# Two penalty passes on ScalarE, 8-bit integers in the dense part, and SyncE's issue of the shift, in a decoder layer on one core

## The chip, the cores and the metric

The kernel runs on one core of one Trainium2 chip. The metric is the device time of one execution in microseconds. Three runs of the kernel before took 790.53 to 792.27 us, median 791.49.

## The reference

Four sequences of 512 rows of 256 values go through a decoder layer with norms behind each part. All arithmetic is in 32-bit floats.

```python
g = sigmoid(x @ Wg + bg)                      # one gate per row
res = (1 - zi) * max(1 - zi - zj, 0) + zi * min(1 - zi + zj, 1)      # zi = g, zj = g of the key
scope = clip((s - 2) ** (1 - g) + 2 - abs(i - j), 1e-32, 1)
log_pen = log(max(res * scope, 1e-32))
x = layernorm(x + softmax(q @ k.T / 4 + log_pen) @ v)                # 16 heads of 16
x = layernorm(x + (softmax(q @ kc.T / 4 + mask) @ vc) @ Wo + bo)     # keys, values of ctx
xq = fake_quant(x)              # round(x / scale) to -128..127, one scale of max|x| for all
h = fake_quant(silu(xq @ wg_q.T) * (xq @ wu_q.T))                    # 704 wide, one scale of max|h|
x = layernorm(x + h @ wd_q.T)
```

The weights of the dense part are rounded to 8-bit integers too, with a scale for each row.

## The kernel before

`make_plan` (L127) writes the order of the attention work out by hand. There are 32 groups, each of four heads of one sequence in self attention (`"s"`) or cross attention (`"c"`). Every group has 16 tiles of 128 x 512 scores twice. Once the queries stand on the partitions, and VectorE takes the maximum of each row (`row_max`, L1003; self attention adds the log penalty `lp` first). Once the keys stand on the partitions, with the negated maxima brought in as twelve more rows of the product, and ScalarE takes the exponential (`exponential`, L890). The product with the values is TensorE's again (`context`, L1552).

A step has 16 slots. In step n the row maxima of group n are taken, slots 0 to 7 hold the second half of group n-2's exponentials and slots 8 to 15 the first half of group n-1's. Other jobs are hung on slots: projections (`q`, `k`, `v`), the gate, the penalties, the two layer norms of a sequence, the preparation of weights. Each engine walks the slots in order and does its part of a job some slots late: ScalarE 0, VectorE 2, GpSimd 1, with exceptions (L47 to L50; a `low` part on GpSimd comes 5 slots late). TensorE is three row-max tiles ahead (three banks of PSUM) and has two banks for exponentials.

The shift: when all maxima of group n are taken, GpSimd splits them in three 16-bit parts (`shift`, L714), TensorE turns them (slot 3), ScalarE copies them to `mT` (L863) and then, at slot 4, issues the DMA that spreads `mT` over the four heads of the query stack `QS` (L868). The exponentials of the group begin at slot 8. SyncE issues everything else: it stores the three parts of a projection to memory (`store_parts`, L521), loads the key and query stacks of the next group from there (L537, L549), and fetches inputs. Its queue in a step is: stacks, fetches, stores of the step's parts (L627 to L644).

Penalties: for each sequence b there are four tiles of 128 x 512. VectorE makes each in seven passes (`penalty`, L1056 to L1083), `PEN_OPS` (L212), one job each. The first two are `pen_a = max(w - z, 0) * w` with w = 1 - zi as a scalar for each partition (L1067, L1069), the next two add `zi * min(z + w, 1)` (L1071, L1073), the last three multiply with the scope and bound it (L1075, L1077, L1079). The tiles of sequence 0 lie in the prologue (`PROLOGUE`, L213), twelve more in the steps. ScalarE takes `Ln` of all four at once (L840). In self attention half of the key tiles add the log by TensorE, and for the other half (`MUL_KT`) GpSimd multiplies the exponentials by the penalty (L711).

The last sequence's output projection is taken apart: `first_half` and `second_half` (L1442, L1449), additions (L1212), statistics, GpSimd's inverse deviation (L687), normalising (L1047), and the maximum of |x| (L1230). `whole_max` (L1258) takes a maximum over partitions through TensorE and makes the scale.

The dense part: `quantise_x` (L1272) rounds x in three passes: multiply and bound below, bound above and add the rounding constant, subtract it (L1053, L1054, L1275). TensorE turns the integers, ScalarE copies them (L922). Gate and up products of 128 x 512 are made for 24 tiles; ScalarE takes silu, VectorE multiplies (L1300) except each third tile, which GpSimd does from ScalarE's copy (`by_pool`, L491; L767), and VectorE takes a maximum of each pair (L1293). The hidden values are rounded in four blocks of 512 rows. Block 0 is VectorE's (`round_h`, L1310, three groups of three passes). Blocks 1 and 2 are ScalarE's in two passes (L961, L954) with a clip by VectorE (`clip_h`, L1319), block 3 is rounded by VectorE (L1348) and finished by ScalarE and a clip. Down products (L1637, L1650), scaling, residual and norm follow for each block.

## Time and profile before

| what | value |
|---|---|
| median of three runs | 791.49 us (790.53 to 792.27) |
| the profiled execution's own time | 788.92 us |
| its span in the profile | 787.1 us |
| TensorE (PE) busy | 659.1 us, 84% |
| VectorE (DVE) busy | 606.4 us, 77% |
| ScalarE (ACT) busy | 492.9 us, 63% |
| GpSimd (POOL) busy | 326.2 us, 41% |
| mean granted TensorE clock | 0.947 |
| chain that ended last | PE 42%, DVE 24%, POOL 14%, ACT 10%, issue 8% |

The span runs from the first to the last instruction; the profiled execution took 1.8 us more than it, and 2.57 us less than the median of the runs. All positions are microseconds from the start of the span. PEld is TensorE's loading of weights, SPq and ACTq are instructions of a queue, such as the issue of a DMA. The granted clock is a share of full speed: 1.0 is 2.4 GHz and 0.5 is 1.2 GHz. The prologue ends near 40 us, the 32 steps near 674 us, and the dense part begins near 710 us.

### The profile page before, as it was taken

How to read it: one execution, taken by the hardware profiler on the slowest of the kernel's cores; microseconds unless marked ns; L12 is line 12 of the kernel's file. 1: busy time of each engine (PE TensorE's matmuls, PEld its weight loads, DVE VectorE, ACT ScalarE, POOL GpSimd, SP SyncE). 2: the span in 40 equal slices, each digit the busy share in tenths (PEclk: the TensorE clock that was granted, in tenths of full speed). 3: DMA queues.
4: the chain of work that ended last, by engine and by line, in shares of the span. 5: the costliest groups of instructions: out<-in, count | busy, mean ns of one | idle time of the engine just before them, and what ended most of it. 6: DMA issues, size and time to landing. Idle time of an engine off the chain costs nothing.

```text
span 787.1 us, 10691 instructions
## 1 busy us (share of the span) xinstructions
PE 659.1 (84%) x3350; PEld 265.6 (34%) x3350; DVE 606.4 (77%) x1574; ACT 492.9 (63%) x807; POOL 326.2 (41%) x414
## 2 busy tenths in 40 slices
PE   7078889999889799998899899999888899956763
PEld 3053223434322243343232443443222243323331
DVE  4888995687899876677998666569985987538997
ACT  4524657556657968654478787455577776944773
POOL 6205866466664414644663144556514001000403
PEclk9688999999999999999999999999999999986975
DMA  2830370220413323321205123322313410000003
GB/s 94 198 110 23 104 175 31 69 65 23 129 41 84 83 70 83 84 70 45 68 23 144 43 60 98 102 58 86 87 40 85 99 43 7 3 1 0 2 0 107
DMA packets 35751, 53.85 MB, mean 68 GB/s; under 512 B 5232, under 2 KB 26736, under 8 KB 35696
## 3 DMA queue, kind: packets, MB, share of 16 engines
q1 hardware_dynamic: 33776, 51.61, 24.7%
q10 hardware_dynamic: 1920, 1.57, 1.3%
q8 instruction: 27, 0.44, 0.2%
q14 instruction: 28, 0.23, 0.1%
HBM read 36.91 MB, written 14.68 MB: 66 GB/s over the span
## 4 chain that ended last, share of the span: by engine, by line
PE 42%; DVE 24%; POOL 14%; ACT 10%; issue 8%; DMA 1%; SPq 0%; POOLq 0%; ACTq 0%; DVEq 0%
POOL probs L711 10%; PE ps L1568 10%; DVE dist L1010 7%; PE ps L1544 7%; PE ps L1521 7%; PE ps L1405 5%; PE ps L1508 5%; ACT probs L900 4%; PE ps L1501 2%; DVE pen_a L1073 1%; PE ps L1548 1%; PE ps L1549 1%; POOL parts L742 1%; DVE h_all L1300 1%; DVE stats L1032 1%
## 5 line engine op out<-in xcount | busy, mean ns | idle before, releaser
L1521 PE MATMUL ps<-KS,QS 96*128 96x512 bf16 x512 | 197.4, 388 | 41.8 <-DVE mx L1010 31.0
L900 ACT ACTIVATE probs<-ps 128x512 f32<-128x512 f32 x256 | 148.9, 597 | 122.6 <-PE ps L1549 91.5
L1010 DVE CUSTOM_DVE_ANT_0 dist<-ps,lp 128x512 bf16<-128x512 f32 x256 | 169.2, 685 | 58.5 <-PE ps L1521 52.8
L711 POOL TENSOR_TENSOR probs<-probs,penT 128x512 f32<-128x512 f32 x128 | 169.7, 1346 | 105.6 <-ACT probs L900 105.6
L1544 PE MATMUL ps<-QS,KS 108*128 108x512 bf16 x512 | 195.3, 384 | 14.6 <-ACT probs L900 11.0
L900 ACT ACTIVATE probs<-ps,mask_col 128x512 f32<-128x512 f32 x256 | 167.0, 690 | 43.8 <-PE ps L1544 40.8
L1010 DVE CUSTOM_DVE_ANT_0 dist<-ps,mask_rest 128x512 bf16<-128x512 f32 x192 | 126.2, 684 | 25.8 <-PE ps L1521 25.6
L1521 PEld LDWEIGHTS ps<-KS,QS 96*128 96x128 bf16 x512 | 50.1, 98 | 189.4 <-DVE mx L1010 122.2
L1568 PE MATMUL ps<-probs,v_s 128*32 128x512 f32 x512 | 68.7, 608 | 16.8 <-POOL probs L711 16.8
L1544 PEld LDWEIGHTS ps<-QS,KS 108*128 108x128 bf16 x512 | 49.8, 98 | 91.2 <-ACT probs L900 58.8
L1568 PE MATMUL ps<-probs,v_c 128*32 128x512 f32 x512 | 68.2, 604 | 0.9 <-ACT probs L900 0.9
L737 POOL TENSOR_TENSOR rest<-proj,parts 128x512 f32<-128x512 f32 x32 | 38.2, 1193 | 72.1 <-ACT parts L807 72.1
L721 POOL TENSOR_SCALAR mrest<-mx 128x16 f32<-128x16 f32 x32 | 9.8, 307 | 103.7 <-DVE mx L1010 103.2
L742 POOL TENSOR_TENSOR parts<-rest,parts 128x512 bf16<-128x512 f32 x32 | 37.8, 1182 | 29.0 <-ACT parts L813 29.0
L1548 PE MATMUL ps<-lpT_hi,ident_h 128*128 128x512 f16 x128 | 48.8, 381 | 0.0
L1549 PE MATMUL ps<-lpT_lo,ident_h 128*128 128x512 f16 x128 | 48.5, 379 | 0.0
L1010 DVE CUSTOM_DVE_ANT_0 dist<-ps,mask_row 128x512 bf16<-128x512 f32 x64 | 42.8, 681 | 7.2 <-PE ps L1521 7.1
L693 POOL TENSOR_SCALAR rstd<-mv 128x4 f32<-128x4 f32 x12 | 2.7, 228 | 104.5 <-DVE mv L1038 104.3
L1010 DVE DVE_READ_ACCUMULATOR2_ANT mx<- 128x1 f32 x512 | 41.6, 81 | 0.0
L807 ACT ACTIVATE proj<-ps,bias_qk 128x512 f32<-128x512 f32 x32 | 22.0, 688 | 20.7 <-PE ps L1405 20.0
L813 ACT ACTIVATE parts<-rest 128x512 bf16<-128x512 f32 x32 | 20.1, 629 | 17.1 <-POOL rest L737 17.1
L1568 PEld LDWEIGHTS ps<-probs,v_s 128*32 128x32 f32 x512 | 10.5, 107 | 42.3 <-issue 42.3
(199 smaller groups left out, 957.7 us busy)
## 6 DMA issues: line engine op xcount, KB each, us to landing
parts_qs<-parts SPq DMA_DIRECT2D x8, 384.0 KB, 2.7
parts_ks<-parts SPq DMA_DIRECT2D x8, 384.0 KB, 2.7
KS<-parts_ks SPq DMA_DIRECT2D x16, 192.0 KB, 3.6
QS<-parts_qs SPq DMA_DIRECT2D x16, 192.0 KB, 4.1
parts_kc<-parts SPq DMA_DIRECT2D x8, 384.0 KB, 2.7
KS<-parts_kc SPq DMA_DIRECT2D x16, 192.0 KB, 3.0
parts_qc<-parts SPq DMA_DIRECT2D x8, 384.0 KB, 2.9
QS<-parts_qc SPq DMA_DIRECT2D x16, 192.0 KB, 3.5
```

What stands on the lines that cost most here:

```text
L711: g.tensor_tensor(probs[:, T % NP, :], probs[:, T % NP, :], penT[:, MUL_KT.index(kt), :], ALU.mult)\
L737: g.tensor_tensor(rest[:, :], proj[:, w % 2, :], parts[:, w % 2, place(job[0], 0), :], ALU.subtract)\
L742: g.tensor_tensor(parts[:, w % 2, place(job[1], 2), :], rest[:, :], parts[:, w % 2, place(job[1], 1), :], ALU.subtract)\
L900: s_.activation(probs[:, T % NP, :], ps[:, exp_bank(T), :], ACT.Exp, bias=bias)\
L1010: v.tensor_tensor_reduce(out=unused[:, (TG * n + i) % AHEAD, :], in0=ps[:, MAX_BANKS[(TG * n + i) % AHEAD], :], in1=lp[:, t, :] if kind == ...
L1405: ins = mm(bank(u), W[what + kind][:, k, c * P:(c + 1) * P], src[:, k, :], start=k == 0, stop=k == HC - 1)
L1508: ins = mm(bank(u)[:, tt * H:(tt + 1) * H], src[:, k, (2 * i + tt) * P:(2 * i + tt + 1) * P], w[:, k, :], start=k == 0, stop=k == HC - 1)
L1521: mm(ps[:, MAX_BANKS[(TG * n + i) % AHEAD], :], QS[0:SK, slot, j, t * P:(t + 1) * P], KS[0:SK, slot, j, :], start=True, stop=True).then_in ...
L1544: ins = mm(o, KS[0:SM, slot, j, kt * P:(kt + 1) * P], QS[0:SM, slot, j, :], start=True, stop=not logged)
L1548: mm(o, ident_h[:, :], lpT_hi[:, k, :], start=False, stop=False)
L1549: ins = mm(o, ident_h[:, :], lpT_lo[:, k, :], start=False, stop=True)
L1568: ins = mm(ps[VC * j:VC * (j + 1), PV_BANK, :], V[kind][:, kt, GH * g + j, :], probs[:, (T + j) % NP, :], start=kt == 0, stop=kt == NT - 1)
```

## The change

Penalties: `PEN_OPS` becomes 5. A new job `relu` on ScalarE, one for each tile, makes `pen_r = Relu(w - z)` and then `pen_r * w` in a buffer of its own; VectorE's second pass now adds it, waiting for `relu_made`, and tells `relu_used`. The `relu` job stands in front of its tile's passes, and in the prologue behind the first part of each projection. Shift: the job `load_m` of ScalarE is gone; SyncE issues the DMA between its loads of the stacks and its fetches and stores. Last norm: two of the four first halves of the projection move to slots before the second half; statistics, inverse deviation, normalising and maximum of the last sequence go in two halves. Integers: `x_clip` and `h_clip` are 8-bit tiles; a multiplication writes into them, with rounding and bounds left to the conversion, and a copy makes them bf16, on VectorE for x, block 1 and the first group of block 0, on ScalarE for the rest. The separate clips are gone. Four scalings of `f_scale` become one (`w_scale` is set to 1 at the start). GpSimd takes nine of the 24 gate/up tiles (1, 3, 6, 8, ... 21) instead of eight.

```diff
@@ make_plan, expand
     if what == "pens":
-        return [("pen", rest[0], t, k) for t in rest[1] for k in range(PEN_OPS)]
+        return [job for t in rest[1] for job in
+                [("relu", rest[0], t)] + [("pen", rest[0], t, k) for k in range(PEN_OPS)]]
...
-            at = [(0, ("shift", s.shift)), (3, ("m", s.shift)), (4, ("load_m", s.shift))] + list(at)
+            at = [(0, ("shift", s.shift)), (3, ("m", s.shift))] + list(at)
...
-    add(at=[(2, ("sigmoids",))])
-    add(at=[(0, ("c2T", B - 1, 1)), (1, ("second_half", B - 1))]
-        + [(2, ("last_x1", B - 1, t)) for t in range(NT)] + [(3, ("x2stats", B - 1, t)) for t in range(NT)],
+    add(at=[(2, ("sigmoids",)), (15, ("first_half_of", B - 1, 2))])
+    add(at=[(0, ("c2T", B - 1, 1)), (0, ("first_half_of", B - 1, 3)), (1, ("second_half", B - 1))]
+        + [(2, (what, B - 1, t)) for t in range(NT) for what in ("last_x1", "x2stats")],
         tasks=[(4, 4, ("ln2", B - 1))])
...
-PEN_OPS = 7
+PEN_OPS = 5
...
+       ("gate", 0, 1), ("reach", 0), ("relu", 0, 0),
+       ("k", "s", 0, 0), ("middle", "k", "s", 0, 0), ("low", "k", "s", 0, 0), ("relu", 0, 1),
+       ("q", "s", 0, 1), ("middle", "q", "s", 0, 1), ("low", "q", "s", 0, 1), ("relu", 0, 2),
+       ("k", "s", 0, 1), ("middle", "k", "s", 0, 1), ("low", "k", "s", 0, 1), ("relu", 0, 3)] \
...
         def by_pool(n):
-            return n % 3 == 2
+            return n % 5 in (1, 3) and n < IT * TC - 2
@@ SyncE
+            def load_shift(n):
+                used(sp, unit[("m", n)])
+                sp.dma_start(QS[SK:SM, n % RING, :, :], mT[:, :].unsqueeze(1).broadcast_to((PARTS * GH, GH, S)))\
+                    .then_inc(shift_loaded, 16)
...
                     for n in s.stacks:
                         load_keys(n)
+                    if s.shift is not None:
+                        load_shift(s.shift)
                     store_parts(now)
...
                     for n in s.stacks:
                         load_stack(n)
+                    if s.shift is not None:
+                        load_shift(s.shift)
                 for what, b in s.fetch:
                     fetch(what, b)
                 store_parts([job for job in jobs if job not in now])
@@ ScalarE
+                elif what == "relu":
+                    b, t = job[1:]
+                    k = NT * b + t
+                    wi, r = w_col[:, t:t + 1], pen_r[:, :]
+                    act.wait_ge(gates_made, b + 1)
+                    if t == 0:
+                        used(act, unit[("gate", b, 1)])
+                    if k:
+                        act.wait_ge(relu_used, k)
+                    s_.activation(r, z_row[:, :], ACT.Relu, bias=wi, scale=-1.0).then_inc(relu_step, 1)
+                    act.wait_ge(relu_step, k + 1)
+                    s_.activation(r, r, ACT.Copy, scale=wi).then_inc(relu_made, 1)
...
-                elif what == "load_m":
-                    n = job[1]
-                    used(act, unit[("m", n)])
-                    act.dma_start(QS[SK:SM, n % RING, :, :], mT[:, :].unsqueeze(1).broadcast_to((PARTS * GH, GH, S)))\
-                        .then_inc(shift_loaded, 16)
...
             act.wait_ge(h_scale_made, 1)
-            for tc in range(1, TC - 1):
-                rounded(tc)
-                integers(tc)
-            integers(TC - 1)
+            rounded(0, H_GROUPS[1:])
+            integers(0, H_GROUPS[1:], 0)
+            for tc in range(2, TC):
+                rounded(tc, H_GROUPS)
+                integers(tc, H_GROUPS, 2 + len(H_GROUPS) * (tc - 2))
@@ VectorE
                 if k == 0:
-                    leave(v.tensor_scalar(pen_a[:, :], z_row[:, :], -1.0, wi, ALU.mult, ALU.add))
+                    leave(v.tensor_scalar(pen_b[:, :], z_row[:, :], wi, 1.0, ALU.add, ALU.min))
                 elif k == 1:
-                    leave(v.tensor_scalar(pen_a[:, :], pen_a[:, :], 0.0, wi, ALU.max, ALU.mult))
+                    dve.wait_ge(relu_made, NT * b + t + 1)
+                    v.scalar_tensor_tensor(pen_a[:, :], pen_b[:, :], zi, pen_r[:, :], ALU.mult, ALU.add)\
+                        .then_inc(relu_used, 1)
...
-                link(round_to(x_round[:, rows, :], x2[:, rows, :], scal[:, 6:7]))
-                v.tensor_scalar(xq[:, rows, :], x_round[:, rows, :], -MAGIC, None, ALU.add).then_inc(xq_made, 1)
+                link(v.tensor_scalar(x_clip[:, rows, :], x2[:, rows, :], scal[:, 6:7], None, ALU.mult))
+                v.tensor_copy(xq[:, rows, :], x_clip[:, rows, :]).then_inc(xq_made, 1)
...
+            def integers(tc, which):
+                cols = slice(tc * 512, (tc + 1) * 512)
+                for lo, hi in which:
+                    m = ISZ[lo]
+                    leave(v.tensor_scalar(h_clip[0:m, lo:hi, cols], h_all[0:m, lo:hi, cols], scal[0:m, 8:9], None, ALU.mult))
+                settle()
+                for lo, hi in which:
+                    m = ISZ[lo]
+                    v.tensor_copy(h_int[0:m, lo:hi, cols], h_clip[0:m, lo:hi, cols]).then_inc(h_ints_by_vector, 1)
...
-            round_h()
-            clip_h(1)
-            for lo, hi in H_GROUPS:
-                h = h_all[0:ISZ[lo], lo:hi, (TC - 1) * 512:TC * 512]
-                v.tensor_scalar(h, h, scal[0:ISZ[lo], 8:9], MAGIC, ALU.mult, ALU.add).then_inc(last_h_rounded, 1)
+            integers(0, H_GROUPS[:1])
+            integers(1, H_GROUPS)
...
-                if tc + 2 < TC:
-                    clip_h(tc + 2)
```

## Rows read from the trace of the kernel before

**Rows 1.** Busy time by stretch (one step each): stretch, length, engines, clock, DMA share, GB/s.

```profile
core 0: us, PE busy (x) PEld busy (x) DVE busy (x) ACT busy (x) POOL busy (x), PEclk, DMA share, GB/s
75.00:98.40 23.40, 19.48 (x96) 6.41 (x92) 21.77 (x47) 14.57 (x26) 19.55 (x19) 1.00 0.29 90
...
120.30:140.90 20.60, 19.26 (x91) 8.75 (x92) 12.48 (x35) 13.52 (x23) 14.50 (x17) 1.00 0.07 22
205.50:227.80 22.30, 17.98 (x97) 5.43 (x96) 21.01 (x51) 10.91 (x19) 13.41 (x14) 1.00 0.47 115
227.80:249.10 21.30, 19.47 (x97) 6.43 (x94) 21.27 (x49) 13.79 (x24) 12.18 (x14) 1.00 0.07 22
...
371.50:392.70 21.20, 17.27 (x92) 5.06 (x88) 21.17 (x51) 10.43 (x18) 12.86 (x13) 1.00 0.25 65
392.70:410.60 17.90, 17.10 (x85) 5.97 (x81) 17.03 (x43) 11.91 (x21) 10.11 (x12) 1.00 0.09 26
```

**Rows 2.** Penalty passes: two groups (busy us, mean ns | idle before), one from the timeline.

```profile
L1069 DVE TENSOR_SCALAR pen_a<-pen_a,w_col 128x512 f32<-128x512 f32 x16 | 13.7, 855 | 0.1
...
L1067 DVE TENSOR_SCALAR pen_a<-z_row,w_col 128x512 f32<-128x512 f32 x16 | 10.0, 623 | 0.1
...
30.55 0.48 DVE L1069 TENSOR_SCALAR pen_a<-pen_a,w_col 128x512 f32<-128x512 f32 x1
```

**Rows 3.** Groups of ScalarE: a pass with a scalar per partition, and the table loads.

```profile
L961 ACT ACTIVATE h_all<-h_all,scal 64x512 f32<-64x512 f32 x2 | 1.4, 708 | 0.0
...
L840 ACT ACT_TABLE_LOAD x4 | 5.1, 1283 | 0.1
```

**Rows 4.** Timeline of the prologue's end: start, duration, engine, instruction, idle before it.

```profile
38.16 1.91 ACT L840 ACTIVATE lp<-pen 128x2048 f32<-128x2048 f32 x1 [4.82 <-DVE pen L1079]
```

**Rows 5.** The shift's issue (ns min/median/max), and stack loads and copy in the timeline.

```profile
L868 ACTq DMA_DIRECT2D QS<-mT x32: 789/790/1402, 58.5 to 679.5; - x32
...
558.38 1.35 SPq L555 DMA_DIRECT2D QS<-parts_qc  x3
...
562.11 0.59 ACT L790 ACTIVATE mT<-ps 12x512 bf16<-12x512 bf16 x1 [0.76 <-PE ps L1468]
```

**Rows 6.** Timeline of the last sequence's norm, 703 to 711 us.

```profile
703.91 0.42 DVE L1212 TENSOR_TENSOR x<-ps,x 128x256 f32<-128x256 f32 x1 [0.86 <-PE ps L1459]
704.37 1.41 DVE L1032 BATCH_NORM_STATS2 stats<-x 128x6 f32<-128x256 f32 x4
...
706.59 1.04 POOL L694 TENSOR_TENSOR rstd<-rstd,minus_half 128x4 f32<-128x4 f32 x1
707.66 1.38 DVE L1047 TENSOR_SCALAR x<-x,mv,rstd 128x256 f32<-128x256 f32 x4 [1.47 <-POOL rstd L694]
709.08 1.22 DVE L1230 TENSOR_REDUCE amax<-x 128x1 f32<-128x1024 f32 x1
```

**Rows 7.** Timeline of the x integers: one of three passes, one of four scalings.

```profile
713.20 0.69 DVE L1054 TENSOR_SCALAR x_round<-x_round 128x1024 f32<-128x1024 f32 x1
...
714.80 0.23 DVE L1280 TENSOR_SCALAR f_scale<-w_scale,scal 128x5 f32<-128x5 f32 x1
```

**Rows 8.** Group of VectorE's gate/up tiles of 128 partitions.

```profile
L1300 DVE SCALAR_TENSOR_TENSOR h_all<-ps,f_scale,silu 128x512 f32<-128x512 f32 x14 | 10.2, 744 | 2.2 <-ACT silu L936 2.2
```

**Rows 9.** Timeline of the hidden integers and down products; last, a stretch with its clock.

```profile
750.67 1.28 DVE L1315 TENSOR_SCALAR h_all<-h_all,scal 128x1536 f32<-128x1536 f32 x1
...
756.86 1.21 DVE L1324 TENSOR_SCALAR h_int<-h_int 128x1536 bf16<-128x1536 bf16 x3
757.99 2.33 DVE L1348 TENSOR_SCALAR h_all<-h_all,scal 128x1536 f32<-128x1536 f32 x3
...
759.88 5.78 ACT L954 ACTIVATE h_int<-h_all 128x1536 bf16<-128x1536 f32 x6
760.23 1.21 DVE L1331 TENSOR_TENSOR y<-ps,out_row 128x1024 f32<-128x1024 f32 x1
...
763.19 3.53 PE L1650 MATMUL ps<-downT,h_int 128*128 128x256 bf16 x24 [0.94 <-DVE h_int L1324]
...
768.41 6.09 PE L1650 MATMUL ps<-downT,h_int 128*128 128x256 bf16 x24 [1.70 <-DVE h_int L1324]
...
768.00:772.00 4.00, 3.59 (x15) 1.81 (x16) 3.93 (x12) 2.08 (x4) 0.70 (x3) 0.52 0.18 65
```

More of the change, by code:

```diff
@@ L56 @@
 EPS = 1e-5
+NORMS = 2 * B + 1
 LOW = -3.0e38
@@ L105, in expand @@
             + [("x2stats", *rest, t) for t in range(NT)]
+    if what == "ln2" and rest[0] == B - 1:
+        return [job for half in range(2) for job in
+                [("x2", *rest, t) for t in range(2 * half, 2 * half + 2)] + [("last_x2max", half)]]
     if what == "ln2":
@@ L391, in decoder_layer @@
         pen_made = sem("penalties_made")
+        relu_step = sem("first_terms_half_made")
+        relu_made = sem("first_terms_made")
+        relu_used = sem("first_terms_used")
         lp_made = sem("log_penalties_made")
@@ L685, in _, with inverse_deviation @@
             chain = norms = 0
-            def inverse_deviation():
+            def inverse_deviation(first=0, last=NT - 1):
                 nonlocal norms
@@ L691, in inverse_deviation @@
                 pool.wait_ge(var_made, norms)
[L692 to L694 removed]
+                k, tiles = norms % 2, slice(first, last + 1)
+                link(g.tensor_scalar(rstd[:, k, tiles], mv[:, k, tiles, 1], EPS, None, ALU.add))
+                g.tensor_tensor(rstd[:, k, tiles], rstd[:, k, tiles], minus_half[:, tiles], ALU.pow).then_inc(rstd_made, 1)
             def link(ins):
@@ L744, in do @@
                         .then_inc(parts_made[w % 2], 1)
+                elif job[0] == "x2stats" and job[1] == B - 1:
+                    if job[2] % 2:
+                        inverse_deviation(job[2] - 1, job[2])
                 elif job[0] in ("x1stats", "x2stats") and job[2] == NT - 1:
@@ L1028, in normalise, with statistics @@
                     .then_inc(side_free[u % 2], 1)
-            def statistics(src, t):
+            def statistics(src, t, first=0, last=NT - 1):
                 ins = v.bn_stats(stats[:, t, :], src[:, t, :])
-                if t == NT - 1:
+                if t == last:
                     link(ins)
@@ L1036, in statistics @@
                     norms[0] += 1
-                    for i in range(NT):
+                    for i in range(first, last + 1):
                         ins = v.bn_aggr(mv[:, k, i, :], stats[:, i, :])
@@ L1216, in do @@
                     leave(v.reciprocal(sig[:, :], sig[:, :]))
+                elif what == "x2stats" and job[1] == B - 1:
+                    b, t = job[1:]
+                    settle()
+                    statistics(x1[:, b % 2, :, :], t, t // 2 * 2, t // 2 * 2 + 1)
                 elif what == "x2stats":
                     b, t = job[1:]
-                    if b < B - 1:
-                        used(dve, *[unit[("wo", b, i)] for i in range(NT // 2)])
-                    elif t == 0:
-                        settle()
+                    used(dve, *[unit[("wo", b, i)] for i in range(NT // 2)])
                     statistics(x1[:, b % 2, :, :], t)
+                elif what == "x2" and job[1] == B - 1:
+                    b, t = job[1:]
+                    n = norms[0] - 1 + t // 2
+                    dve.wait_ge(rstd_made, n)
+                    leave(v.tensor_scalar(x2[:, NT * b + t, :], x1[:, b % 2, t, :], mv[:, n % 2, t, 0:1],
+                                          rstd[:, n % 2, t:t + 1], ALU.subtract, ALU.mult))
+                elif what == "last_x2max":
+                    half = job[1]
+                    settle()
+                    tiles = slice(NT * (B - 1) + 2 * half, NT * (B - 1) + 2 * half + 2)
+                    v.tensor_reduce(amax[:, B - 1 + half:B + half], x2[:, tiles, :], AX.XY, ALU.max,
+                                    apply_absolute_value=True).then_inc(x2_max, 1)
                 elif what == "x2":
@@ L1448, in do @@
                         mm(ps[:, WO_BANKS[t], 0:H], c2T[:, 0, t * P:(t + 1) * P], W["o"][:, 0, :], start=True, stop=False)
+                elif what == "first_half_of":
+                    t = job[2]
+                    pe.wait_ge(exp_done, TG * len(groups))
+                    mm(ps[:, WO_BANKS[t], 0:H], c2T[:, 0, t * P:(t + 1) * P], W["o"][:, 0, :], start=True, stop=False)
                 elif what == "second_half":
```

94 lines of the change are left out of this document (36 added, 58 removed), and 3 rows, old and new, of the table PROLOGUE.

## The prediction

> **What bounds the kernel now.** I first cut the attention part into its steps: a new one begins at every sixteenth row maximum of VectorE (L1010), and for each stretch I compare the busy time of the engines with its length [rows 1]. The steps that compute penalties beside the row maxima are VectorE's: 371.5 to 392.7 us is 21.2 us long with VectorE busy 21.17, 205.5 to 227.8 has 21.01 of 22.3, 227.8 to 249.1 has 21.27 of 21.3, while TensorE is busy only 17.3 to 19.5 and ScalarE 10.4 to 13.8. A step without penalties (120.3 to 140.9) turns this round: TensorE 19.26 of 20.6, VectorE 12.48. So VectorE time is worth up to its full length in the eight of 32 steps that hold penalties, and little in a step like the last. Then comes the dense tail from 699 us on (last layer norm, x integers, gate/up loop, hidden integers, last norm), read from the timeline; there a chain of short VectorE passes sets the end, with TensorE, GpSimd and ScalarE fed in between [rows 6 to 9].
>
> **Two penalty passes to ScalarE.** What goes are L1067 and L1069, 16 of each, mean 623 and 855 ns [rows 2]: 1.48 us a tile. One such pass alone takes 0.48 us [rows 2]; the mean is higher, which I put down to GpSimd's work beside it. Added on ScalarE are a Relu and a Copy, each from SBUF with a per-partition scalar. The nearest form in the trace is L961 on 64x512, 708 ns [rows 3]. With the wait between the two I take 1.45 us a tile. Bounds: 1.2 us if each costs no more than the copy of m (0.59 [rows 5]); 1.6 us with a longer wait.
>
> In the prologue (four tiles) ScalarE gets 5.8 us more, minus some 0.7 us of short waits that it fills. Before the Ln it sat idle 4.82 us [rows 4], waiting for the last penalty. That idle time goes, VectorE is done some 5 us earlier, and the Ln starts between 0.5 us earlier and 1 us later: I take 0, and ScalarE replaces VectorE as what is late.
>
> In the loop there are twelve tiles. Two-tile steps lose 2.96 us of VectorE work. Where TensorE had over 3.5 us to spare I count nearly all of it: 2.7 us (205.5), 2.7 (371.5), 2.5 (75.0). The step at 227.8 has TensorE busy 19.47 of 21.3, so 2.0. The step at 392.7, with one tile and TensorE at 17.10 of 17.9, gives 0.9. Three more steps hold one tile each and have VectorE less than full: 0.6 each, under half of 1.48. Sum 12.6. Against it stand twelve pairs of 1.45 us in ScalarE's in-order queue, with exponentials and the q/k copies behind them. TensorE waits for an exponential to give back one of two banks, so a pair can hold it. The cover is that ScalarE is about half idle there [rows 1] and VectorE has three banks of scores in hand; I let 15% through, 2.6 us. Net **10.0 us**. The ends are 17.7 (12 tiles at 1.48, nothing through) and 2 (most of the pair on the path). The new wait of VectorE on `relu_made` stands behind its row maximum; the relu job has its slot one job ahead, plus VectorE's lag of two slots, so it costs nothing unless ScalarE falls four slots behind. ScalarE's own wait on `relu_used` is for a pass that is eight slots old in a two-tile step.
>
> The trace's rows give 0.48 us on VectorE undisturbed against about 0.7 on ScalarE for the same pass. The Trainium skill ("ScalarE: Activation LUTs", rules for kernel authors) says to keep relu and mul on VectorE, which is up to about 3 times faster. By that rule the move is a loss; it is my slower rival below, since the rows say that VectorE is the full engine in these steps.
>
> **SyncE issues the shift.** L868 holds ScalarE's queue 0.79 us, 32 times [rows 5], though most of that lies beside an activation of 0.6 us that is already running. What is left, 0.2 us, makes at most 32 x 0.2 = 6.4 us of ScalarE, on the path only where ScalarE is late: I take **1.0 us**. The same DMA still has to land. In SyncE's queue the wait for the copy of m now stands behind the six stack loads and in front of the fetches and the stores of that step's parts. The loads are long issued by then: in the step at 554.7 the last group of loads starts at 558.38, for 1.35 us, and the copy of m only at 562.11 [rows 5]. Low parts come at slot 5 or later, behind m at slot 3, so stores wait for nothing new; fetches go out up to 8 us later and are used one step or more later. Bounds 0 to 3 us gained; if a shift came late, see the rivals.
>
> **The tail.** (1) Last output projection and norm. Two of the eight halves of the projection run ahead of c2T's second half, and the statistics go in halves. The last addition now ends at 704.33; with less on TensorE in front of it, it is bounded by VectorE's own add plus statistics (0.42 and 0.35, four times), which I put 1.0 us earlier. From there to the end of the maximum at 710.30 stood 1.41 us of statistics, the power on GpSimd (1.04), 1.38 of normalising and 1.22 of maximum [rows 6]. Behind the last addition stays one statistic of four (1.06 less), and half of the normalising and of the maximum (0.69 and 0.61 less): 2.4. Together **3.4 us**.
> (2) x integers: three passes of some 0.7 us become two, and the second chunk releases TensorE, so 2 x 0.69; four f_scale instructions of 0.2 become one, 0.65 [rows 7]. **2.0 us**.
> (3) Gate/up: VectorE makes 15 tiles instead of 16 at 744 ns [rows 8], but the loop's first three slots now give it two tiles instead of three, and it idles there; the rest is 13 tiles and 11 maxima, as before. 0.
> (4) Hidden integers. VectorE had nine passes and the clips and roundings of other rows before the first scaling at 760.23 [rows 9]. Now it has two passes of 1.28 and 1.22 us for one group, then three roundings (2.33 for all) and three copies (about 2.2): 7.1 us from 750.67, so 757.8, and the first down product is there about 758. Gain 2.3. The two clips of 1.21 us between the scalings go too, with 0.3 us that one waits: 2.7. ScalarE makes as many passes as before in an order that ends some 0.7 us later (766.4 for 765.66); from there TensorE needs 6.1 us for the last 24 products [rows 9] at the low clock (0.52 granted in 768 to 772), to 772.5. VectorE wants its second half at 772.8. Just covered. **5.0 us**. The 8-bit passes show nowhere; I take the duration of the float ones. If they ran at the 1.2 us per 1,024 elements of a maximum, the tail would lose 5 us; the other end is no gain over float.
> Tail: 3.4 + 2.0 + 0 + 5.0 = **10.4 us**, between 4 and 12.
>
> **Sum.** 10.0 + 1.0 + 0 + 10.4 = 21.4 us. The profiled execution took 788.92 us (span 787.1 and 1.8 around it), so it would come to 767.5. The median of the runs is 791.49, 2.57 above; from it the same sum gives 770.1.
>
> **Rivals.**
> - *ScalarE takes back much of the relief.* The pair falls between a q/k copy and its middle part, TensorE is held, and the loop gains 3 us instead of 10. For it: ScalarE is the one whose exponentials release TensorE, and in the step at 227.8 it has 13.8 us of work already. Against: half idle elsewhere. 777.1 us.
> - *The relief is worth all of VectorE's time*, 17.7 us, with less disturbance between VectorE and GpSimd besides. For: three steps with VectorE at 94 to 100%. Against: TensorE's 81 to 91% in them. 762.4 us.
> - *Slower: the pair lies wholly on the path.* Place: ScalarE's queue in the penalty steps, exponentials behind the pair, TensorE at its two banks, VectorE's relief eaten by waiting for scores. Price 12 x 1.45 = 17.4 us against 11.4 gained elsewhere: 797.5 us. It decides from 0.95 us of each pair on the path with no relief. Against: TensorE has waited for VectorE, not for ScalarE, in these steps. This is what the rule named above would make of it.
> - *The change does not do what it says*: Relu calls for its own table. A load takes 1,283 ns [rows 3], two a tile make 41 us. Exp, Copy and Identity follow each other in the trace without one, and I hold it for one in a hundred, inside the slower chance. The Trainium skill ("ScalarE: Activation LUTs", table sets) says that relu sits in every set; no row here shows a Relu.
> - *Tail held by TensorE's clock.* Were the low clock to last through the three later down products, each takes 6.1 us instead of 3.5 [rows 9] and point (4) gains nothing: 775.1 us.
>
> **Chances.** Forecast 0.66; ScalarE takes back 0.15; full relief 0.08; clock in the tail 0.06; slower 0.05. A difference under 0.2% (1.6 us) is about what cannot be told from none; almost nothing lies there. Range 760 to 780: from full relief with the tail's upper bound to the first rival with 3 us more lost in the tail. Faster 0.93, same 0.02, slower 0.05.
>
> **What would show it.** In the changed profile: the steps with two tiles near 19 us with VectorE still the fullest engine; Relu and Copy near 0.7 us without a table load; the Ln in the prologue near 38 us with ScalarE busy up to it; TensorE's shift wait not longer; 3.4 us less from the last projection to the maximum of x, 2.0 less to the first gate product, 5.0 less from the scaled `out_row` to the end. Wrong would be: penalty steps as long as before with TensorE waiting for ScalarE, or 8-bit passes over 1 us per 1,024 elements.

## The result, and the profile after

The changed kernel took 782.89 us in the median of four runs (781.85 to 783.49), beside 791.88 for the kernel before: ratio 0.988 (95%: 0.985 to 0.991). Timed again later (change_again below), the ratio was 0.992 (0.990 to 0.995). So it is some 6 to 10 us faster. The forecast was 21.4 us faster, 770.1, with a range of 760 to 780: the result lies above it.

The profiled execution took 781.85 us, with a span of 780.1 (before 787.1). From the start of the last step's row maxima (661.0 before, 663.3 after) to the end it is 9.3 us shorter, for 10.4 forecast. Everything ahead of that point is 2.3 us **longer**, for 11.0 us shorter forecast. The forecast failed in the attention part.

Stretches of the changed kernel, one step each; they answer to [rows 1], in the order 75.0, 120.3, 205.5, 227.8, (the step behind it), 371.5, 392.7:

```profile
core 0: us, PE busy (x) PEld busy (x) DVE busy (x) ACT busy (x) POOL busy (x), PEclk, DMA share, GB/s
76.60:101.10 24.50, 20.11 (x96) 6.57 (x100) 18.85 (x44) 16.68 (x30) 20.21 (x20) 1.00 0.32 99
123.40:144.10 20.70, 19.29 (x91) 8.75 (x92) 12.56 (x37) 13.49 (x23) 14.53 (x17) 1.00 0.22 61
210.10:231.80 21.70, 17.25 (x93) 5.68 (x96) 18.92 (x46) 13.15 (x23) 13.27 (x14) 1.00 0.46 118
231.80:252.10 20.30, 18.58 (x94) 6.12 (x90) 18.10 (x46) 14.78 (x27) 10.81 (x12) 1.00 0.07 22
252.10:269.70 17.60, 16.84 (x88) 5.33 (x88) 14.38 (x42) 15.56 (x27) 7.02 (x10) 1.00 0.44 130
375.50:395.30 19.80, 16.10 (x88) 5.29 (x88) 19.31 (x47) 12.56 (x22) 12.43 (x13) 1.00 0.26 70
395.30:413.90 18.60, 17.80 (x89) 5.96 (x81) 14.81 (x41) 13.10 (x23) 10.08 (x12) 1.00 0.09 26
```

VectorE did get its relief: in the step at 210.1 it is busy 18.92 of 21.7 us, where before it was 21.01 of 22.3. But the step is hardly shorter, and now no engine is full in it. The step at 252.1 holds no penalty and is 1.0 us longer than its counterpart before (16.6 us).

Who waited for whom in two penalty steps, first of the kernel before (205.5 to 249.1), then of the changed one (210.1 to 252.1): total us, times, longest.

```profile
PEld ps L1521 <- DVE mx L1010: 11.6, 15, 1.1
POOL probs L711 <- ACT probs L900: 11.3, 3, 4.1
...
PEld ps L1544 <- ACT probs L900: 2.7, 6, 0.7
```

```profile
POOL probs L732 <- ACT probs L931: 11.5, 4, 3.8
...
PEld ps L1569 <- ACT probs L931: 5.7, 12, 0.9
PE ps L1593 <- POOL probs L732: 3.9, 4, 1.2
...
PEld ps L1546 <- DVE mx L1037: 3.6, 5, 0.8
DVE dist L1037 <- PE ps L1546: 3.5, 7, 0.9
```

TensorE's wait for VectorE's maxima fell from 11.6 to 3.6 us. In its place stand waits for ScalarE's exponentials (up from 2.7 to 5.7) and for GpSimd's multiplies (up from 1.7 to 3.9), and VectorE waits for TensorE (3.5, for 0.9). The new operations, from the page's groups:

```profile
L869 ACT ACTIVATE pen_r<-pen_r,w_col 128x512 f32<-128x512 f32 x16 | 11.6, 722 | 0.5
L867 ACT ACTIVATE pen_r<-z_row,w_col 128x512 f32<-128x512 f32 x16 | 11.5, 716 | 0.0
```

The prologue's end, ScalarE's timeline (answers to [rows 4]):

```profile
30.43 0.71 ACT L867 ACTIVATE pen_r<-z_row,w_col 128x512 f32<-128x512 f32 x1
31.17 0.72 ACT L869 ACTIVATE pen_r<-pen_r,w_col 128x512 f32<-128x512 f32 x1
31.92 5.50 ACT L855 ACTIVATE KS<-own_rows 32x2048 bf16<-32x2048 bf16 x3
37.44 1.28 ACT L877 ACT_TABLE_LOAD   x1
38.74 1.91 ACT L877 ACTIVATE lp<-pen 128x2048 f32<-128x2048 f32 x1
```

ScalarE is busy without a gap up to the Ln; VectorE had made its last penalty at 34.6 us.

The tail, VectorE's and TensorE's timelines (answers to [rows 6, 7, 9]):

```profile
708.21 0.69 DVE L1261 TENSOR_REDUCE amax<-x 128x1 f32<-128x512 f32 x1
...
711.01 0.75 DVE L1314 TENSOR_SCALAR x_clip<-x,scal 128x1024 int8<-128x1024 f32 x1
711.80 0.69 DVE L1315 CAST xq<-x_clip 128x1024 bf16<-128x1024 int8 x1
...
747.65 1.28 DVE L1350 TENSOR_SCALAR h_clip<-h_all,scal 128x1536 int8<-128x1536 f32 x1
748.96 1.23 DVE L1354 CAST h_int<-h_clip 128x1536 bf16<-128x1536 int8 x1
750.11 2.31 DVE L1350 TENSOR_SCALAR h_clip<-h_all,scal 128x1536 int8<-128x1536 f32 x3
752.45 2.15 DVE L1354 CAST h_int<-h_clip 128x1536 bf16<-128x1536 int8 x3
755.76 1.23 DVE L1361 TENSOR_TENSOR y<-ps,out_row 128x1024 f32<-128x1024 f32 x1 [1.17 <-PE ps L1665]
```

```profile
755.59 7.04 PE L1681 MATMUL ps<-downT,h_int 128*128 128x256 bf16 x48
762.96 3.52 PE L1681 MATMUL ps<-downT,h_int 128*128 128x256 bf16 x24 [0.33 <-ACT h_int L988]
```

### The profile page after: what moved, and what is told of

Same layout as the page of the kernel before. It is cut to its first block, busy times and chain, and to the rows that moved or that the text cites. A ratio compares the mean times of both kernels' runs of the same rounds, so it can differ in the third digit from the quotient of the medians.

```text
span 780.1 us, 10707 instructions
## 1 busy us (share of the span) xinstructions
PE 659.0 (84%) x3348; PEld 267.6 (34%) x3350; DVE 574.5 (74%) x1523; ACT 511.0 (66%) x841; POOL 326.4 (42%) x417
## 4 chain that ended last, share of the span: by engine, by line
PE 46%; POOL 16%; DVE 14%; ACT 12%; issue 10%; DMA 2%; SPq 0%; POOLq 0%; DVEq 0%; ACTq 0%
POOL probs L732 12%; PE ps L1593 10%; PE ps L1546 8%; PE ps L1569 8%; PE ps L1533 5%; PE ps L1430 5%; ACT probs L931 5%; DVE dist L1037 4%; PE ps L1526 3%; POOL rest L758 1%; PE ps L1573 1%; PE ps L1574 1%; PE ps L1446 1%; POOL parts L763 1%; DVE x L1214 1%
## 5 line engine op out<-in xcount | busy, mean ns | idle before, releaser
L732 POOL TENSOR_TENSOR probs<-probs,penT 128x512 f32<-128x512 f32 x128 | 167.2, 1325 | 107.9 <-ACT probs L931 107.9
L1037 DVE CUSTOM_DVE_ANT_0 dist<-ps,mask_row 128x512 bf16<-128x512 f32 x64 | 42.9, 683 | 10.4 <-PE ps L1546 10.3
L714 POOL TENSOR_SCALAR rstd<-mv 128x4 f32<-128x4 f32 (+1 forms) x13 | 3.0, 232 | 98.6 <-DVE mv L1065 98.5
L837 ACT ACTIVATE parts<-rest 128x512 bf16<-128x512 f32 x32 | 20.1, 629 | 17.8 <-POOL rest L758 17.8
```

The costliest lines, as they stand in the source:

```text
L732: g.tensor_tensor(probs[:, T % NP, :], probs[:, T % NP, :], penT[:, MUL_KT.index(kt), :], ALU.mult)\
L1037: v.tensor_tensor_reduce(out=unused[:, (TG * n + i) % AHEAD, :], in0=ps[:, MAX_BANKS[(TG * n + i) % AHEAD], :], in1=lp[:, t, :] if kind == ...
```

## The experiments

All were timed in five rounds beside the kernel before; ratios are to it, with 95% intervals. "us" is the median. Where two ratios are compared below, their difference is given in us of the kernel before's 791. Four of the kernels leave work out and so compute something else: relief_alone and loop_relief (a term of the penalty), relief_few_mul and passes7_few_mul (three of four multiplies, the first of them that term too).

| label | us | ratio |
|---|---|---|
| pens_only | 794.75 | 1.0053 (1.0028 to 1.0079) |
| shift_only | 790.01 | 0.9984 (0.9964 to 1.0005) |
| tail_only | 781.82 | 0.9880 (0.9853 to 0.9907) |
| no_pens | 780.74 | 0.9869 (0.9842 to 0.9896) |
| relief_alone | 780.23 | 0.9852 (0.9821 to 0.9884) |
| pair_alone | 783.57 | 0.9910 (0.9878 to 0.9941) |
| passes7_few_mul | 748.80 | 0.9464 (0.9430 to 0.9498) |
| relief_few_mul | 743.18 | 0.9392 (0.9360 to 0.9424) |
| relu_quiet | 785.76 | 0.9932 (0.9905 to 0.9959) |
| half_quiet | 782.53 | 0.9915 (0.9888 to 0.9942) |
| ln_first_quiet | 781.89 | 0.9891 (0.9858 to 0.9924) |
| pens_shift | 793.72 | 1.0035 (1.0019 to 1.0051) |
| ln_first | 783.39 | 0.9898 (0.9880 to 0.9915) |
| seven_ln_first | 779.71 | 0.9871 (0.9848 to 0.9894) |
| prologue_only | 775.44 | 0.9810 (0.9780 to 0.9840) |
| not_batch1 | 780.95 | 0.9861 (0.9839 to 0.9883) |
| loop_relief | 774.18 | 0.9808 (0.9772 to 0.9844) |
| change_again | 785.13 | 0.9924 (0.9900 to 0.9949) |

### The change in its parts

**pens_only**, **shift_only** and **tail_only** add one part to the kernel before; **no_pens** is the changed kernel without the penalty move; **pens_shift** is the kernel before with both attention parts.

```diff
 # no_pens: the first two passes back on VectorE, no relu job
-PEN_OPS = 5
+PEN_OPS = 7
```

> The kernel before with the penalty move alone. Between the two traces the attention part was 2.3 us longer and the tail 9.3 us shorter. Theory 1 (ScalarE's pair lies on the path and takes the relief back, or more): 1 to 4 us slower than before, with PE waiting for probabilities in the penalty steps. Theory 2 (VectorE's relief is worth little, because exponential, GpSimd's multiply and context product set these steps, and the pair costs nothing either): within 1 us of before. The sum on record wanted 10.0 us faster.

> The kernel before with only the issue of the shift's DMA moved to SyncE. Forecast on record: 1.0 us faster (0 to 3). Theory 3 (the shift's move is what costs the attention part its 2.3 us, since it now stands behind loads in SyncE's queue): 2 to 3 us slower. Otherwise within 1 us of before or up to 3 us faster.

> The kernel before with only the dense tail changed (last norm in halves, 8-bit integers, GpSimd's share, one f_scale pass). Sum on record: 10.4 us faster. From the two traces, measured from the start of the last row-maximum step: 9.3 us faster, so about 782.5 us.

> The changed kernel with all seven penalty passes on VectorE again. Theory 1 (pair on the path): 1 to 4 us faster than the changed kernel, 779 to 782 us, better than both. Theory 2 (relief worth nothing, pair free): within 1 us of the changed kernel's 782.9. The sum on record would make it 10 us slower.

> The kernel before with the penalty move and the shift's move, without the tail: the changed kernel's attention part. By itself the penalty move measured 4 us slower and the shift's move 1.3 us faster (790.9 to 790.0 in medians). If they simply add: 793 to 794 us. If the shift's move pays for part of the pair, because its 0.79 us no longer stands in ScalarE's queue near it: 791 to 792.5 us.

The tail is worth 1.2%, 9.5 us: all that the change gains. The shift's move gives 1.3 us, not told from nothing. The penalty move makes the kernel before **slower** by 0.5% (4 us), with the shift's move beside it 0.35%; the changed kernel's two timings (0.9879, 0.9924) lie above no_pens (0.9869), the second clear of its interval, the first not. So the part from which 10 us were expected costs 1 to 4.

### Relief and price apart

```diff
 # relief_alone: no pair on ScalarE, the add reads another buffer
-                [("relu", rest[0], t)] + [("pen", ...
+                [("none", rest[0], t)] + [("pen", ...   # keeps the passes' slots
...
-                    dve.wait_ge(relu_made, NT * b + t + 1)
-                    v.scalar_tensor_tensor(pen_a[:, :], pen_b[:, :], zi, pen_r[:, :], ...)
+                    v.scalar_tensor_tensor(pen_a[:, :], pen_b[:, :], zi, z_row[:, :], ...)
 # pair_alone: the pair stays, VectorE makes seven passes
-PEN_OPS = 5
+PEN_OPS = 7
```

> The changed kernel without the Relu and Copy on ScalarE: VectorE keeps its five passes and adds z_row where the first terms stood, so the penalties leave out the term w_i*max(w_i - z_j, 0). It has VectorE's relief and pays nothing on ScalarE. Measured: 780.74 us with seven passes on VectorE, 782.9 with the change. Theory 1 (ScalarE's pair takes back a relief that is there, as the 12.6 us of the record): 768 to 772 us. Theory 2 (the relief is worth little, since exponential, GpSimd's multiply and context product set these steps): 777 to 781 us, within 3 us of the version with seven passes.

> The changed kernel with the pair on ScalarE kept and VectorE making all seven passes as before, so the pair's result is not used: the price of the pair alone, against 780.74 us without it. Theory 1 (a large relief taken back): 788 to 792 us. Theory 2 (small relief, small price): 781 to 784 us.

Against no_pens the relief alone gives 1.3 us (ratios 0.9869 and 0.9852), the pair alone costs 3.2 us; each lies within the intervals. Both hold the prologue's four tiles too: the first row maximum comes at 36.0 us in relief_alone, at 40.0 in no_pens and at 42.2 in pair_alone. The times are as Theory 2 said of the relief, but they don't even show those 4.0 us of lead; the mean granted clock of relief_alone's runs is 0.945 to 0.951, that of no_pens' 0.949 to 0.953. The traces say more, since a step whose granted clock is 1.00 mostly repeats to 0.1 us: change_again's trace has eight of the changed kernel's nine lengths below again, and 25.7 us for the step at 76.6, where its clock was 0.93. The table has nine steps that hold penalties or stand behind one that does, all at 1.00, lengths in us (by the change's positions; the step at 55.0 is left out, since its clock differs, and those at 123.4 and 413.9, which kept their 20.7 and 18.2 us):

| kernel | 76.6 | 101.1 | 210.1 | 231.8 | 252.1 | 326.2 | 352.4 | 375.5 | 395.3 | sum |
|---|---|---|---|---|---|---|---|---|---|---|
| before | 23.4 | 21.8 | 22.3 | 21.3 | 16.6 | 26.5 | 23.0 | 21.2 | 18.0 | 194.1 |
| relief_alone | 23.2 | 22.3 | 21.4 | 19.9 | 17.6 | 26.1 | 23.0 | 19.7 | 18.5 | 191.7 |
| changed | 24.5 | 22.3 | 21.7 | 20.2 | 17.6 | 26.2 | 23.0 | 19.8 | 18.7 | 194.0 |

The relief is 2.4 us (12.0 forecast in these steps), the pair takes back 2.3 (2.6 forecast), 1.3 of it in the one step at 76.6. Relieved steps do get shorter (231.8: 1.4 us, 375.5: 1.5), but the step behind each gets longer (1.0 and 0.5): the row maxima ran ahead, and then stand and wait. In pair_alone, where VectorE makes all seven passes, the eight steps from 101.1 on sum to 170.6 us, and so they do in no_pens: there the pair costs nothing in the loop at full clock, and 2.2 of its 3.2 us are the prologue's.

So the 2.3 us by which everything ahead of the tail got longer are not in these nine steps (194.1 and 194.0). The first row maximum comes 0.6 us later, the two steps behind it take 1.0 us more at a granted clock of 0.74 for 0.84, and the step at 165.1, without penalties, takes 21.6 us at 0.92 for 20.1 at 1.00; 0.8 us come back at 536.4 and 555.1.

### Is GpSimd's multiply the cap?

```diff
-                if e and groups[e[0]][0] == "s" and e[1] // GH in MUL_KT:
+                if e and groups[e[0]][0] == "s" and e[1] // GH in MUL_KT and e[1] % GH == GH - 1:
```

> relief_alone with three of four multiplies of GpSimd left out (the last of each four is made; the other probabilities go without their penalty). To be held against passes7_few_mul. Theory 2 (GpSimd's multiply stands between the exponential and the context product and caps the penalty steps): with that cap gone VectorE's relief shows, this kernel is 6 us or more faster than passes7_few_mul, and penalty steps get down to 17 to 19 us. Rival (TensorE or ScalarE caps them): under 3 us between the two.

> Seven penalty passes on VectorE, no pair on ScalarE, three of four multiplies of GpSimd left out. Against 780.74 us with all multiplies. Theory 2: VectorE is the only bound left in the penalty steps and they stay near 21 us or shrink only as its passes get shorter without GpSimd beside them; relief_few_mul is 6 us or more below. Rival: both kernels within 3 us of each other.

The two differ by 5.6 us, but the first row maximum alone is 4.4 us earlier in relief_few_mul (35.5 for 39.9). That much is the prologue. The nine steps sum to 175.9 us with seven passes and 173.1 with five: 2.8 us, hardly more than with all multiplies. So the multiplies make these steps 18 us longer, but they are not what makes the relief worthless. Two steps of each, seven passes first:

```profile
196.30:214.80 18.50, 17.03 (x96) 5.21 (x92) 18.07 (x50) 10.69 (x19) 4.54 (x8) 1.00 0.39 95
353.00:371.90 18.90, 17.22 (x96) 5.17 (x88) 18.86 (x51) 10.40 (x19) 4.46 (x8) 1.00 0.27 73
```

```profile
189.60:206.50 16.90, 16.83 (x96) 5.55 (x90) 16.48 (x46) 10.75 (x19) 4.03 (x8) 1.00 0.42 103
344.10:361.50 17.40, 16.71 (x96) 5.34 (x88) 17.37 (x46) 10.45 (x19) 4.07 (x8) 1.00 0.30 79
```

In the step at 189.6 TensorE is busy 16.83 of 16.9 us: where GpSimd is out of the way, TensorE takes over within 1.6 us of the 18.5 with seven passes. In the step at 344.1 VectorE stays the full engine, and there its relief shows whole: 1.5 us less for 1.49 us less of work. My Theory 2 was half right: in most steps there is a next engine close behind, not GpSimd alone.

### Where the pair stands

```diff
 # relu_quiet
-                [("relu", rest[0], t)] + [("pen", rest[0], t, k) for k in range(PEN_OPS)]]
+        return [("pen", rest[0], t, k) for t in rest[1] for k in range(PEN_OPS)]
...
+    for b in range(1, B):
+        for t in range(NT):
+            ... steps[k].items[6].append(("relu", b, t)), or slot 14 or 15 of the step before
```

> The changed kernel with the pair's slots in the loop moved: from slots 0, 7 and 8 (where the exponentials begin that GpSimd multiplies) to slots 6, 14 and 15. Prologue as in the changed kernel. If the pair's price (3 us measured by itself) comes from standing ahead of these exponentials: 1.5 to 3 us faster than the changed kernel's 782.9, and the first two exponentials of the third penalty step stand 0.6 us apart again instead of 1.9. Rival (the price is ScalarE's time itself, wherever it stands, or the prologue's): within 1 us of 782.9.

In the changed kernel the second pair of the step at 76.6 stands behind the first exponentials of a group, where GpSimd waits to multiply:

```profile
94.49 0.74 ACT L867 ACTIVATE pen_r<-z_row,w_col 128x512 f32<-128x512 f32 x1
95.27 0.72 ACT L869 ACTIVATE pen_r<-pen_r,w_col 128x512 f32<-128x512 f32 x1
95.89 0.58 ACT L931 ACTIVATE probs<-ps 128x512 f32<-128x512 f32 x1
```

Moving it did as was asked of these two exponentials (0.6 us apart again) and the kernel got slower, if anything: 785.76 us. The pair now stood ahead of another exponential. The edit did one thing more, which I had overlooked: with the relu jobs gone from the list, the penalty passes were dealt over the slots anew (those of a first tile stand at 0, 1, 3, 4, 6 for 1, 2, 4, 5, 6). The step at 101.1 is 23.5 us for 22.3, but loop_relief below, with the same slots and no pair in the loop at all, has 23.2 there: most of that is the passes' own place. Held against loop_relief, the pair costs 1.5 us in the six steps that are at full clock in both; in its old place it cost 0.9 in the same six (changed kernel against relief_alone). So that the price comes from a bad slot is not borne out; that it is ScalarE's time ahead of exponentials, wherever it stands, is what is left, and not shown by itself.

### The prologue

```diff
 # ln_first (on the change), ln_first_quiet (on relu_quiet), seven_ln_first (on no_pens)
-    + [("own_rows", r) for r in range(1, RING)] \
     + [job for job in expand(("pens", 0, range(NT))) if job[0] == "pen"] + [("ln", 0)] \
+    + [("own_rows", r) for r in range(1, RING)]
 # half_quiet: tiles 0 and 1 of the prologue with seven passes on VectorE
```

> relu_quiet with two tiles of the prologue back on VectorE (seven passes) and two on ScalarE. In the prologue ScalarE then loses 2.9 us ahead of the Ln and VectorE gains some 3; relief_alone had the first row maximum 4.0 us earlier, the change 0.7 us later than seven passes. If ScalarE's queue alone holds the Ln: the Ln comes 2 us or more earlier and the whole is 1.5 to 2.5 us faster than relu_quiet. If not: within 1 us of relu_quiet.

> relu_quiet with the Ln of the prologue ahead of ScalarE's three copies of constant rows (5.50 us together) instead of behind them. In the changed kernel VectorE made its last penalty at 34.6 us and the Ln began at 38.74, straight behind these copies. If that is what turns the prologue's relief into nothing: the Ln begins near 34.7, the first row maximum near 36.7, and the whole is 3 to 4.5 us faster than relu_quiet. Rival (what follows needs the rows, or the exponentials behind the copies start later by as much): within 1 us of relu_quiet.

> The changed kernel with only the prologue's Ln put ahead of the three 1.8 us copies of constant rows. In the quiet-slot version this gave 3.2 us. If the copies held the Ln in the changed kernel: the Ln begins near 34.7 us for 38.74, the whole is 3 to 4.5 us below 782.9, 778.5 to 780. If not: 782 to 784.

> Seven passes on VectorE everywhere, no pair, and the Ln ahead of the constant rows: the control. With seven passes VectorE's last penalty ends near 38.0 us and is what the Ln waits for, so the order on ScalarE should give nothing: 780 to 781.5 us, as the version with seven passes. If the copies by themselves delay something else, 777 to 779.

With the Ln first, the changed kernel's ScalarE and VectorE meet there:

```profile
31.52 1.28 ACT L877 ACT_TABLE_LOAD   x1
34.30 1.91 ACT L877 ACTIVATE lp<-pen 128x2048 f32<-128x2048 f32 x1 [1.51 <-DVE pen L1105]
36.24 5.50 ACT L855 ACTIVATE KS<-own_rows 32x2048 bf16<-32x2048 bf16 x3
```

The Ln begins 4.4 us earlier. That the copies held the Ln is settled by these rows; ln_first_quiet gained 3.2 us on relu_quiet, with intervals that overlap, and the control with seven passes stayed with no_pens (0.9871 and 0.9869), so that there VectorE's last penalty is what is late. half_quiet failed as a test: its second pair stood 3.54 us waiting until VectorE had read the one buffer, so the Ln came at 39.17 us, no earlier; its 1.3 us less than relu_quiet lie within the intervals. But **ln_first** itself gained nothing that can be told from the change (0.9898 beside 0.9879 and 0.9924). In its profile the 5.3 us of lead at the second step are still 5.0 us at the fourth and 6.5 at 263.2, and gone by the last step (0.9 us). Most of it, 4.6 us, goes in two steps that hold no penalty at all, first of the change and then of ln_first:

```profile
536.40:555.10 18.70, 17.36 (x86) 6.28 (x83) 17.76 (x53) 11.19 (x21) 12.09 (x15) 1.00 0.28 90
```

```profile
531.00:554.70 23.70, 20.13 (x90) 7.41 (x87) 23.36 (x51) 13.01 (x23) 15.78 (x17) 0.93 0.23 76
...
554.80:573.70 18.90, 17.24 (x90) 5.53 (x88) 15.29 (x44) 10.03 (x18) 6.15 (x9) 0.91 0.41 100
```

The granted clock fell to half in part of each of ln_first's two. Ahead of the second fall TensorE had stood for 3.00 us behind a row maximum:

```profile
554.28 0.39 PE L1546 MATMUL ps<-KS,QS 96*128 96x512 bf16 x1 [3.00 <-DVE mx L1037]
```

```profile
554.80:558.80 4.00, 4.00 (x16) 0.93 (x15) 1.95 (x8) 0.60 (x1) 0.00 (x0) 0.57 1.03 248
```

From 8 us behind the first row maximum to the last step the traces have three to seven such falls, near 275 us in each kernel with all multiplies, the others not always in the same steps. The scatter of the runs goes with the mean clock: of the eight runs of change_again the fastest is 781.77 us at 0.951 and the slowest 787.67 at 0.943.

### The loop by itself, with the better prologue

All three have ln_first's prologue. **prologue_only** makes seven passes in the loop, **loop_relief** five without a pair, **ln_first** five with the pair; **not_batch1** takes only batch 1's four tiles back.

```diff
+def moved(b, t):
+    return b == 0          # prologue_only;  b != 1 in not_batch1
 # loop_relief: as ln_first, the relu jobs of b >= 1 gone, z_row added in place of pen_r
```

> ln_first with the pair in the prologue alone and seven passes on VectorE in the loop. At equal clock the loop's twelve tiles summed to 0.1 us between seven passes and the change. If the loop's relief and price cancel: within 1 us of ln_first; by the trace's steps 776.5 to 779. If the loop's relief is worth what was forecast: 8 us or more slower than ln_first.

> ln_first with only batch 1's four tiles back on VectorE. At a clock of 1.00 their steps (76.6 and 101.1 us) had grown by 1.0 and 0.5 us, while the steps of batches 2 and 3 summed to 1.6 us less. If these add: 1 to 2 us faster than ln_first, 776 to 778 us, the best of all. Rival (steps trade with their neighbours, nothing is left of it): within 1 us of ln_first.

> ln_first with the twelve pairs of the loop left out: VectorE makes five passes there and adds z_row where the first terms stood, so the penalties of batches 1 to 3 leave out the term w_i*max(w_i - z_j, 0). The prologue is that of ln_first and prologue_only. Against prologue_only (775.4, seven passes in the loop) this is the loop's relief by itself; against ln_first (783.4) it is the price of the loop's pairs. By steps at a clock of 1.00: relief 2.4 us and price 2.3 us, so 773 to 776 in the median. By the forecast's relief of 12.6 us: 763 us.

> The changed kernel as it is, timed beside loop_relief. 782 to 784 us in the median. If the scatter of its runs goes with TensorE's mean granted clock, runs at 0.947 are some 1 to 4 us above runs at 0.952.

prologue_only is 775.44 us, ratio 0.981 (0.978 to 0.984): **faster than both kernels**, some 15 us below before and 5 to 9 below the change. I had expected 776.5 to 779, or ln_first within 1 us, and it is 7 us by ratio below ln_first. Its own trace comes from one of the slower of its six runs (780.16 us at a clock of 0.947): the lead on seven_ln_first, 4.3 us at the first row maximum, is 0.4 us at the last step there.

loop_relief has the same ratio (0.9808), and its nine steps sum to 193.3 us: the relief in the loop is worth nothing that can be told. From it to ln_first the twelve pairs seem to cost 7 us by ratio. But the two differ in the slots of the passes too, and in the eight steps from 101.1 on, at full clock in both, loop_relief takes 170.2 us and ln_first 169.5: no price. In their traces nearly all of the 8.6 us between them at the last step lies in four steps where ln_first's granted clock is the lower one: 3.1 us in the third step (0.87 for 1.00), 1.0 in that at 425.7 (0.85 for 0.92), 4.6 in the two shown above (531.0 and 554.8). Their runs differ likewise (loop_relief 0.954 in the mean, ln_first 0.948). Whether the pairs bring on such falls is open.

not_batch1 gained 3 us on ln_first, its interval just touching it, and not the best.

## Why the prediction was wrong

**Step that failed: "Where TensorE had over 3.5 us to spare I count nearly all of it ... Sum 12.6."** Measured: 2.4 us in nine steps at full clock, of 12.0 forecast for them, and 0 to 1.3 us in the times (relief_alone, loop_relief). Term by term, of the 2.7 us at 205.5 the trace of relief_alone has 0.9, of the 2.7 at 371.5 1.5, of the 2.5 at 75.0 0.2, of the 2.0 at 227.8 1.4, and the 0.9 at 392.7 became 0.5 us more. VectorE's work did go: its penalty passes in the twelve tiles sum to 74.0 us before and 54.0 after, more than the 17.7 that I had counted. I read "VectorE busy 21.17 of 21.2 us" [rows 1] as "the step ends when VectorE is done, and what TensorE has to spare is free to take". But a step's length is measured from row maximum to row maximum, and these run a step ahead of their group's exponentials: relief moves that border, and the next step gives part of it back (the table above). And what follows the exponentials had its own length, which I had not added up. The chain of waits over the two steps names the successor, before and changed:

```profile
by line: DVE dist L1010 39.6%; DVE pen_a L1073 10.6%; DVE pen_a L1077 8.6%; DVE pen_a L1069 6.8%; DVE pen_b L1071 6.6%; DVE pen_b L1075 6.4%; DVE pen_a L1067 6.1%; DVE pen L1079 3.9%; POOL probs L711 2.8%; PE ps L1568 2.4%; issue 1.2%; DVE 
```

```profile
by line: POOL probs L732 30.0%; issue 18.8%; ACT probs L931 10.5%; PE ps L1593 8.7%; PE ps L1569 5.3%; PE ps L1430 4.6%; PE ps L1546 3.6%; ACT pen_r L867 3.2%; POOL rest L758 3.1%; ACT parts L831 2.2%; ACT parts L837 1.5%; ACT oT L907 1.5%;
```

Before, hardly anything but VectorE is on it, and yet its relief was worth a fifth of the forecast: a chain shows what was late, not how close the next one is. One link of the changed kernel's chain in full:

```profile
225.38 0.62 ACT pen_r L867
226.05 0.60 issue
226.65 0.59 ACT probs L931
227.30 4.08 POOL probs L732 x3
231.52 1.06 PE ps L1593 x8
```

The pair, the exponential behind it, three multiplies, the value product: 7.2 us from the pair's start to the product's end, with VectorE nowhere in it. relief_few_mul shows that thinning the multiplies does not free the relief by itself either (2.8 us in the nine steps). That TensorE is as close behind is shown in one step (189.6); how much of the missing 9.6 us each chain takes is not measured.

**The pair's price, 2.6 us**: 2.3 in the changed kernel's steps at full clock, nothing in pair_alone's eight; not shown wrong. Each pass took 0.72 us, and no table load stands near it, as said. With the loop's gain near zero the first rival, "ScalarE takes back much of the relief" (777.1), comes nearest, but for another reason: the relief was not there to be taken. The rule of the Trainium skill that I set beside the slower rival ("ScalarE: Activation LUTs", rules for kernel authors, relu and mul on VectorE) had the right sign for the move as a whole. Its factor of up to about 3, though, is given for bf16, which I had left out; in this kernel's 32-bit floats a pass took 0.72 us on ScalarE and 0.49 on VectorE undisturbed. A second page of the Trainium skill ("Perfetto Trace Analysis", Optimizing Scalar/DVE Operations) says that work may move to ScalarE where VectorE is saturated; here it was, at 94 to 100% of a step, and the move gained nothing. The measurement decides: saturated in a stretch is not enough.

**The prologue, 0**: right, by the mechanism given (Ln at 38.74 for "near 38", ScalarE busy up to it). What I missed is that 5.50 us of that queue needn't stand ahead of the Ln; prologue_only puts them behind it and gains 4.8 us by ratio on seven_ln_first, which has the same order and no pair. There the pair pays: VectorE works alone in front of one late consumer, and ScalarE has room.

**The shift, 1.0 us**: 1.3 (interval from 2.8 gained to 0.4 lost), not shown wrong.

**The tail, 10.4 us**: 9.5 by tail_only, 9.3 in the trace. To the end of the maximum of x 3.7 us (45.6 from the last step's start, 49.3 before) for 3.4; to the first hidden pass 1.6 for 2.0; from there to the end 4.0 (32.4 for 36.4) for 5.0. The missing 1.0 us is in one row: the first scaling stood 1.17 us behind TensorE's down products and came 8.1 us after the first pass, not 7.1. I had counted VectorE's passes but not TensorE's 5.4 us for block 0. The 8-bit passes cost what float passes did (0.75 and 0.69 us a chunk, 1.28 and 1.23 for 1,536 elements), as taken. The clock rival was wrong: the last down products took 3.52 us.

That the whole range missed comes from the penalties alone: its slow end was drawn with 3 us gained in the loop and 3 us lost in the tail. The tail lost 1, but the penalty move cost 1 to 4 us, which lies below even the sum's own bound of 2 gained.

## What to carry to other kernels

An engine that fills a stretch is worth relieving only down to the next chain there. Before counting TensorE's spare time, add up the other dependency chains of the stretch (here exponential, four multiplies, product) and cut the gain to the difference. If maxima or loads run a step ahead, sum over the steps behind as well. A pass is best moved where one engine works alone before one late consumer, such as a prologue, and then look what else stands in the consumer's queue.

## What the runs showed of the hardware

Beside GpSimd's multiplies VectorE's passes got longer. The same line with all multiplies (no_pens), then with a quarter of them:

```profile
L1081 DVE SCALAR_TENSOR_TENSOR pen_a<-pen_b,z_col,pen_a 128x512 f32<-128x512 f32 x16 | 18.3, 1142 | 0.1
```

```profile
L1081 DVE SCALAR_TENSOR_TENSOR pen_a<-pen_b,z_col,pen_a 128x512 f32<-128x512 f32 x16 | 16.3, 1018 | 0.1
```

Undisturbed in the prologue it took 0.75 us. The Trainium skill ("SBUF — State Buffer", Terms) says that VectorE and GpSimd take turns on a shared port pair, the loser blocked for a whole instruction; these rows agree in direction, but no row shows how long a pass was held. With two passes gone, some of the remaining ones got longer (the scope's add on L1101 981 ns, 833 as L1083 in no_pens) and one shorter (the add on L1097 790 ns, 1,142 as L1081). Together a tile's passes in the loop fell from 6.17 to 4.50 us, 1.67 for the 1.48 forecast, so this disturbance does not explain the missing gain.

TensorE's granted clock fell to 0.5 for a few us at three to seven places of the steps, and where it did varies between kernels that do the same work there: the step at 536.4 took 18.7 us at 1.00 and 23.7 at 0.93. A gain of 4 us early in this kernel can be gone by such falls later, and only the times of many runs, or steps compared at equal clock, tell it.
